# A graph network in seven edge passes on one core: the steps between the passes moved into the phases beside them

## What is computed

```python
h = relu(layernorm(x)); x = x + clip(h + segment_sum(h[src] * edge_weight * weight, dst) + 0.1 * h, 0, 1)
h = relu(layernorm(x)); x = x + tensor_product_layer(h, edge_attr_8, ...)     # sums over src
h = relu(layernorm(x)); x = x + segment_sum(einsum('ei,eio->eo', h[src], W_rel[type]) * e, dst)
h = relu(layernorm(x))
w = kernel_net(edge_attr_6).reshape(-1, 16, 16)                               # one 16x16 matrix per edge
for i in range(4):
    agg = segment_sum(einsum('ei,eio->eo', h[src], w), dst) * inv_deg
    h = gelu(agg + h @ root_W[i] + root_b[i])
x = x + h
```

## Time and profile before

| quantity | value |
|---|---|
| median of 3 runs | 26,634.41 us (26,603.08 to 26,652.0) |
| the profiled execution, its time | 26,617.11 us |
| its span, first to last instruction | 26,615.3 us |
| PE busy | 20,719.2 us (78%) |
| DVE busy | 19,332.0 us (73%) |
| ACT busy | 13,734.7 us (52%) |
| POOL busy | 19,283.0 us (72%) |
| mean granted TensorE clock | 0.884 |

### The profile page before, as it was taken

One profiled execution on the slowest core, in us unless ns is written; L12 is line 12 of the kernel. 1 busy time (PEld: TensorE's weight loads), 2 busy tenths in 40 slices (PEclk: granted clock), 3 DMA queues, 4 the chain that ended last, 5 costly groups with the idle time before them and its releaser, 6 DMA issues. The chain is left out here.

```text
span 26615.3 us, 414978 instructions
## 1 busy us (share of the span) xinstructions
PE 20719.2 (78%) x124290; PEld 13265.2 (50%) x124290; DVE 19332.0 (73%) x31590; ACT 13734.7 (52%) x14669; POOL 19283.0 (72%) x17673
## 2 busy tenths in 40 slices
PE   5777738888885888885888888588886888778886
PEld 2333326666653444443444444466664666556664
DVE  5555537777775777775777777688886888778886
ACT  4666601111112555553222222588886888778885
POOL 5777758888884666665777777677776777767776
PEclk9888968888887999997888888799997999889998
DMA  2222235555552222221333333466664666556664
GB/s 46 42 41 42 40 65 91 93 93 93 92 91 53 63 62 62 62 63 47 118 118 119 118 117 119 124 177 179 177 171 132 179 176 177 147 155 179 178 177 123
DMA packets 2209937, 2929.13 MB, mean 110 GB/s; under 512 B 979092, under 2 KB 1694178, under 8 KB 2182118
## 3 DMA queue, kind: packets, MB, share of 16 engines
q1 hardware_dynamic: 1250178, 2311.22, 29.5%
q0 software_dynamic: 814208, 166.54, 9.4%
q10 hardware_dynamic: 145440, 450.17, 4.4%
HBM read 2252.13 MB, written 674.06 MB: 110 GB/s over the span
## 5 line engine op out<-in xcount | busy, mean ns | idle before, releaser
L601 POOL DMA_INDIRECT got<-table,idx x14746 | 14929.0, 1012 | 6026.9 <-issue 4434.6
L778 PE MATMUL in_place<-place_hot,tparts 128*128 128x320 bf16 (+1 forms) x63408 | 11225.5, 338 | 2420.8 <-ACT place_hot L954 2420.7
L778 PEld LDWEIGHTS in_place<-place_hot,tparts 128*128 128x128 bf16 x63408 | 6449.6, 104 | 6568.0 <-ACT place_hot L954 2716.6
L949 ACT ACTIVATE near<-place_b,far_lanes 128x640 bf16<-128x640 f16 (+1 forms) x9180 | 6302.8, 771 | 216.8 <-DMA place_b<-place_row 216.3
L1087 DVE TENSOR_REDUCE msg<-prod 128x64 f32<-128x1024 f32 x4040 | 4906.8, 1215 | 103.3
L954 ACT ACTIVATE place_hot<-near,one 128x5760 bf16<-128x5760 bf16 (+1 forms) x1020 | 4805.9, 4712 | 33.2
L1454 POOL DMA_INDIRECT added<-add_rows,add_idx x2222 | 3690.9, 1661 | 766.2 <-issue 617.6
L1079 DVE TENSOR_TENSOR prod<-w_in,got 128x1024 f32<-128x1024 f32 x2424 | 2913.4, 1222 | 695.8 <-DMA got<-table,idx 580.6
L939 ACT ACTIVATE outb<-run 128x256 f32<-128x256 f32 (+1 forms) x1010 | 737.6, 730 | 4124.9 <-DVEq L1124 4124.9
L1497 PE MATMUL acc<-hot,spread 128*128 128x392 bf16 x12120 | 2399.1, 352 | 0.0
L890 ACT ACTIVATE h<-h1p,b 128x512 f32<-128x512 f32 x808 | 544.3, 686 | 2682.5 <-DVE wcopy L1072 2544.4
(11 more groups left out here) (253 smaller groups left out, 17587.0 us busy)
## 6 DMA issues: line engine op xcount, KB each, us to landing
w_in<-kept SPq DMA_DIRECT2D x2424, 512.0 KB, 3.3
kept<-wcopy ACTq DMA_DIRECT2D x808, 512.0 KB, 2.7
got<-table,idx POOLq DMA_INDIRECT x14746
attr<-in_edge_attr SPq DMA_DIRECT2D x202, 1024.0 KB
rows<-in_src_row SPq DMA_DIRECT2D x202, 704.0 KB
sums<-outb SPq DMA_DIRECT2D x1010, 128.0 KB
place_b<-place_row SPq DMA_DIRECT2D x612, 160.0 KB
range_b<-range_row SPq DMA_DIRECT2D x609, 160.0 KB
```

The lines of the kernel that those rows point to most:

```text
L601: pool.indirect_dma_start(out=dst[:, j * width:(j + 1) * width], out_offset=None, in_=table, in_offset=bass.IndirectOffsetOnAxis(ap=idx[:, ...
L778: mm = pe.matmul(in_place[b][:, h, :], tparts[:, s, t, :], place_hot[:, b, t, h * XC:(h + 1) * XC], start=(t == 0 and s == 0), stop=(t == ...
L949: act.activation(near[:, t, :], place_b[:, b, :], ACT.Abs, bias=SB["far_lanes"][:, t:t + 1]).then_inc(S["near_made"], 1)
```

## The change

The changed program differs in five places:

- `root_rows` is gone. Its transposes, copies and matmuls stand in `collect`, on PE and DVE, behind the mending of the carried rows, for each of the four depths. The bias `root_b` is added by the last instruction of a block, which was a copy.
- `table_parts` is gone. The edge pass loads the table into `rows` (a tile that exists already) and DVE splits it inside the pass's phase, ahead of its first `pick`; PE waits for `parts_made` before its first sums.
- SP issues the indices of chunks 0 and 1 first in a pass, then places and ranges, then the 13 loads of the table.
- `sum_unsorted` is one phase with both groups of features and the turning in it, behind one jump.
- `node_update_3` works in two halves of 784 columns, without the addition of the bias, and SP stores each half of the table as soon as its gelu is made. The table of depth 0 is stored once ahead of the loop. After the last depth nothing is stored.

```diff
         layernorm(nc, SB)
+        store_table(nc, h, table16)
         for depth in range(DEPTH):
-            root_rows(nc, SB, depth)
-            store_table(nc, h, table16)
             edge_pass(nc, a, SB, "kernel_kept" if depth else "kernel_net", table16)
-            collect(nc, SB, sums16, D)
+            collect(nc, SB, sums16, D, depth)
             sum_unsorted(nc, a, SB, sums16, D)
-            node_update_3(nc, SB, depth)
+            node_update_3(nc, SB, table16 if depth < DEPTH - 1 else None)
...
# edge_pass
-            table_parts(nc, table, tparts)
+            whole = SB["rows"][:, 0:KT * P].rearrange("p (t c) -> p t c", t=KT)
+            table_v = table.rearrange("(o r) f -> r o f", o=OWNERS)[:, :, 0:D]
...
+                def load_whole():
+                    sp.wait_ge(S["whole_clear"], 1)
+                    for t in range(KT):
+                        w = min(P, RANGE - t * P)
+                        sp.dma_start(whole[0:w, t, :].rearrange("r (o f) -> r o f", o=OWNERS), table_v[t * P:t * P + w, :, :]).then_inc(S["whole_in"], 16)
...
+                for k in range(2):
+                    load_idx(k, k, 0, k)
                 if X:
                     load_places(0, 0)
                     load_places(1, 1)
                     load_ranges(0, 0)
-                for k in range(2):
-                    load_idx(k, k, 0, k)
+                    load_whole()
...
# PE, ahead of the first in_place_sums
+                    pe.wait_ge(S["parts_made"], 1)
...
# DVE
+                def split_table():
+                    dve.wait_ge(S["whole_in"], 16 * (KT))
+                    c = Chain(dve, S["whole_step"])
+                    c.step(dve.tensor_copy(tparts[:, 0, :, :], whole[:, :, :]))
+                    for s in range(1, PIECES):
+                        c.step(dve.tensor_tensor(whole[:, :, :], whole[:, :, :], tparts[:, s - 1, :, :], ALU.subtract))
+                        c.step(dve.tensor_copy(tparts[:, s, :, :], whole[:, :, :]))
+                    dve.sem_inc(S["parts_made"], 1)
+
                 if X:
                     for b in range(HALVES):
                         hot_rows(b, b, 0)
+                    split_table()
                     pick(0, 0, 0)
...
# collect, PE
+                for n in range(BLOCKS):
+                    c0, places, w = blockwise(n)
+                    if n >= 2:
+                        pe.wait_ge(taken, n - 1)
+                    pe.transpose(pt[n % 2][0:w, :], h[:, c0:c0 + w], SB["ident"][:, :]).then_inc(turned_p, 1)
+                    pe.wait_ge(turned_s, n + 1)
+                    pe.matmul(pz[n % 2][:, 0:w], hT[0:w, n % 2, :], SB["bd_root"][0:w, depth, 0:w], start=True, stop=True).then_inc(mapped, 1)
...
# node_update_3
+            for n in range(2):
+                qs, cols = slice(n * HALF, (n + 1) * HALF), slice(n * HALF * D, (n + 1) * HALF * D)
+                dve.tensor_tensor(..., bcast(SB["inv_deg"][:, qs], 2, D), ALU.mult).then_inc(scaled, 1)
+                dve.wait_ge(scaled, n + 1)
+                dve.tensor_tensor(tmp[:, cols], tmp[:, cols], agg[:, cols], ALU.add).then_inc(summed, 1)
...
+                act.activation(h[:, cols], tmp[:, cols], ACT.Gelu_apprx_tanh).then_inc(made, 1)
...
+                sp.wait_ge(made, n + 1)
+                sp.dma_start(table.rearrange("(p q) f -> p (q f)", p=P)[:, cols], h[:, cols]).then_inc(stored, 16)
```

More of the change, by code:

```diff
@@ L446, in _ @@
                 dve.tensor_copy(range16[:, :], own[:, :]).then_inc(made, 1)
[L449 to L472, removed]
 def relation_weights(nc, a, SB):
@@ L978, in _ @@
                 early = 2
+                if X:
+                    dve.memset(whole[:, KT - 1, :], 0.0).then_inc(S["whole_clear"], 1)
                 dve.memset(run[:, 1, :, :], 0.0).then_inc(S["run_cleared"], 1)
@@ L1200, in _ @@
                 dve.wait_ge(carried, 1)
-                dve.tensor_tensor(fixed[:, :], fixed[:, :], carry[:, :], ALU.add).then_inc(fix_made, 1)
+                dve.tensor_tensor(fixed[:, :], fixed[:, :], carry, ALU.add).then_inc(fix_made, 1)
+                if depth is None:
+                    return
+                for n in range(BLOCKS):
+                    c0, places, w = blockwise(n)
+                    dve.wait_ge(turned_p, n + 1)
+                    if n >= 2:
+                        dve.wait_ge(mapped, n - 1)
+                    dve.tensor_copy(hT[0:w, n % 2, :], pt[n % 2][0:w, :]).then_inc(turned_s, 1)
+                    dve.wait_ge(mapped, n + 1)
+                    dve.tensor_tensor(tmp[:, c0:c0 + w].rearrange("p (q f) -> p q f", f=D), pz[n % 2][:, 0:w].rearrange("p (q f) -> p q f", f=D),
+                                      bcast(SB["root_b"][:, depth, :], 1, places), ALU.add).then_inc(taken, 1)
             @block.gpsimd
@@ L2076, in node_update_3 @@
[L2076 to L2080 removed]
+def node_update_3(nc, SB, table):
+    h, tmp, agg = SB["h"], SB["tmp"], SB["agg"]
+    HALF = NQ // 2
+    with phase(nc, "scaled", "summed", "made", "stored") as (block, scaled, summed, made, stored):
         @block.vector
         def _(dve):
[L2083 to L2086 removed]
+            for n in range(2):
+                qs, cols = slice(n * HALF, (n + 1) * HALF), slice(n * HALF * D, (n + 1) * HALF * D)
+                dve.tensor_tensor(agg[:, cols].rearrange("p (q f) -> p q f", f=D), agg[:, cols].rearrange("p (q f) -> p q f", f=D),
+                                  bcast(SB["inv_deg"][:, qs], 2, D), ALU.mult).then_inc(scaled, 1)
+                dve.wait_ge(scaled, n + 1)
+                dve.tensor_tensor(tmp[:, cols], tmp[:, cols], agg[:, cols], ALU.add).then_inc(summed, 1)
@@ L2088, in _ @@
         @block.scalar
         def _(act):
-            act.wait_ge(summed, 1)
-            act.activation(h[:, :], tmp[:, :], ACT.Gelu_apprx_tanh).then_inc(act_step, 1)
+            for n in range(2):
+                cols = slice(n * HALF * D, (n + 1) * HALF * D)
+                act.wait_ge(summed, n + 1)
+                act.activation(h[:, cols], tmp[:, cols], ACT.Gelu_apprx_tanh).then_inc(made, 1)
+        @block.sync
+        def _(sp):
+            if table is None:
+                return
+            for n in range(2):
+                cols = slice(n * HALF * D, (n + 1) * HALF * D)
+                sp.wait_ge(made, n + 1)
+                sp.dma_start(table.rearrange("(p q) f -> p (q f)", p=P)[:, cols], h[:, cols]).then_inc(stored, 16)
+            sp.wait_ge(stored, 32)
```

257 lines of the change are left out of this document (132 added, 125 removed).

## The result

| quantity | before | after |
|---|---|---|
| median (range) | 26,627.75 us (26,603.08 to 26,652.0; 4 runs) | 26,463.57 us (26,443.72 to 26,474.75; 4 runs) |
| the profiled execution, its time | 26,617.11 us | 26,473.86 us |
| its span | 26,615.3 us | 26,472.1 us |
| mean granted TensorE clock | 0.884 | 0.883 |

A forecast was written before the change was run, and what follows sets the result against it. POOL's gathers were taken to bound the weighted and kept passes, PE and DVE the relational one, with serial gaps between. Terms summed to 206.8 us off 26,617.1, giving 26,410; forecast 26,420 us, range 26,380 to 26,475.

The forecast's parts named there:

- Update, root map and store: Three gaps ahead of kept passes: update to next phase falls from 31.7 to 9.4 us, saving 66.9 us in all.
- Depth 0: Root map of depth 0, gelu's end to the store: 20.1 us, of which one 1.0-us boundary remains, saving 19.1 us.
- the last depth: Last update to final add: the node update shrinks from 7.0 to 4.6 us, saving 2.4 us.
- Table split, passes that POOL bounds: Three kept passes and the weighted one: POOL starts earlier by 87.8 us, less 10 for held gathers, net 77.8.
- the slower rival: Kept passes: POOL's gathers are held longer throughout; doubled hits would add 720 us, giving 27,130; chance 0.03.
- Table split, relational pass: The relational pass follows PE, which would start 20.2 instead of 33.6 us into the phase, saving 13.4 us.
- General sums: After collecting, six calls: eight jumped phases fewer at 3.4 us each, saving 27.2 us.
- the passes follow DVE: Rival, kept and weighted passes: they move with the first product, gaining 55.6 us instead of 77.8; 26,432 us; chance 0.12.
- the one phase costs what all did: Rival, general sums: the single phase costs as much as all before, so 27.2 us are missing; 26,438 us; chance 0.05.
- the signs named for a wrong prediction: A kept pass changing by over 10 us, POOL waiting for a slot, or the gap after collecting staying at 17 us.
- the first two rivals: Passes following DVE (chance 0.12) and one general-sums phase costing what all did (0.05); both together 26,460 us.

The follow-up runs named there:

- gaps_only_again: Changed kernel with the edge passes, table split and general sums of the kernel before: 26,559.47 us, ratio 0.997 to the kernel before.
- split_only_again: Kernel before with only the new edge pass (indices first, table split inside the pass): 26,574.56 us, ratio 0.9979 to the kernel before.
- Late indices: Changed kernel with SP's first two index loads moved behind the table loads: 26,492.76 us, ratio 0.9947 to the kernel before.

## Why the prediction held, and where it was wrong

**Update, root map and store** held: 69.8 us for 66.9. The gap from update to next phase is 7.9 us instead of the 9.4 costed, three times; the 31.7 us it had before were read from the last gap, and the other two had 30.8 and 31.1, which takes 1.5 us back. The four half instructions and the second half of gelu took 4.8 us from first start to last end (the sum: 4.6); the store with its boundary took the rest, 3.2 us, as the first half leaves while the second is made. `gaps_only_again` shows the same 8 us with the old passes, so it belongs to this part. Depth 0 (19.3 for 19.1) and the last depth (2.2 for 2.4) held too.

**Table split, passes that POOL bounds.** Each step inside the pass came as said: first gather 2.4 to 3.1 us into the phase (2.4), PE at 20.3 to 21.3 (20.2), no wait for a slot, and each subtraction holding one gather, by 1.0 to 1.75 us (1.98 to 2.69 against 0.94). With the gather that met the first cast that is 3.2 to 4.0 us a pass, 14.8 in the four, where 10 were taken. The Trainium skill (GPSIMD Engine Reference, Specifications) names DVE instructions with two SBUF inputs, or in a 2-port perf mode, as what GpSimd contends with; the subtractions agree, and the gather that began 0.27 us ahead of the first cast took 1.41 us, which is 0.47 more than usual and near the 0.4 that the prediction reckoned for a cast if it counted (0.41 to 0.85 at this place in the five passes with a split). For the kept passes the term was 57.9 and gave 52.0 (70 in `split_only_again`): right within the wander. The step that failed is the unspoken one behind all of it, that **a pass from first gather to last stays as long as it was**. In the weighted pass 975 ns a gather became 983, 20.2 us over 2,424 gathers (3.6 of them the split's), which ate the gain of the earlier start. The prediction had looked for such holding only in the kept passes and under `prod`, as the slower rival.

**Table split, relational pass.** "It follows PE" gave 13.4 us. PE did start 12 us sooner, and in `split_only_again`, at the old step, the pass ended 19.3 us sooner after the start of its phase. In the changed kernel the pass took 24 us more from first `picked` to last, by the slower step (0.17 us over all 202 chunks would be 34; the first chunks of the kernel before were not at 19.63 either), and so ended 11.8 later. What the term said of PE's start was right; that the pass's step would stay was not.

**General sums**: 27.2 was costed and 18.2 came. The step that failed is "Two phases cost 6.8 us, one 3.4", and with it "I take the whole, because a jump over either of today's bodies is in the same average": the average was over 5.1 and 1.8. The reading of SP's waits that was to confirm it had divided 4.6 us by two, where the two waits are 4.0 and 0.6. Merging takes the turning phase from a call with 16 features, 1.7 to 1.9 us and 3.2 in the last, and two turnings and one sums phase from the relational one, 8.4 to 8.8: by these rows of the kernel before some 19 us. The gaps shrank by 1.0 to 1.9 us at four calls, 4.0 at the last and 8.5 at the relational layer.

**The rivals.** That the passes follow DVE is out: POOL waits for "issue" alone. Late indices cost 20 to 29 us in the medians, and 12 in the profile of the weighted pass, which agrees but would not prove it. That the one phase costs what all did is out: 5.1 to 5.3 us for 6.8 and for 13.7; yet most of the 6.8 us stayed, and in four of the six calls the gap shrank by only 1.0 to 1.9 us where 3.4 were costed. The slower one is out for the kept passes, at 1.051 to 1.054 us a gather against 1.048 to 1.053 before; it is the right mechanism for the weighted pass, at 8 ns instead of the 31 from which it turns the sign. Of the signs named for a wrong prediction one came: the kept passes changed by 6, 4 and 12 us from first gather to last, and the last of them oversteps the bound of 10, which was narrower than the wander of the same code. POOL never waited for a slot, and the gaps after collecting were 15.3 to 16.9 us, where 14 were forecast and 17 would have been no gain.

That the median lies inside the range, 11 us from its upper end, is in part luck: that end was set where the first two rivals hold, and neither did. What filled the room was the passes' own wander, which the sum had put at nothing.

## What to carry to other kernels

Serial steps between phases can be costed to a few us from one timeline, and moving them under a cover that is idle pays in full. A pass that repeats a chunk 200 times can't: 0.1 us a chunk in how two engines fall against each other is 20 us, as much as what an earlier start brings, so put the wander of the pass (here 10 to 20 us each, seen in code that no edit touches) into the range, ahead of any finer argument. A phase that is jumped over can cost 5.1 us or 1.8 by what lies behind the jump, so read each by itself, and not the mean: merging two saved the cheaper one.

## What the runs showed of the hardware

- The same kernel took 26.6 thousand us on some chips and 33.8 on others; there PE issues single matmuls with 1.2 to 2.4 us between them in the rows shown, behind the first 45 of a pass. The change was worth the same share on both (0.9938 and 0.9923, with intervals that overlap).
- A gather of 0.94 us that began under a 1.89-us subtraction of two SBUF operands lasted up to 2.69, to 1.2 us beyond the subtraction's end. Under the small `place_hot` one-hot tiles of the weighted pass the price was 0.006 us a gather on average before and 0.09 after.
- Of two phases that all engines jump over, the one with the large body took 4.9 to 5.3 us and the one with the small body 1.7 to 1.9; PE's branch took 3.3 to 3.8 us of the first and 0.24 of the second.
- The relational pass has two steady steps, 19.63 and 19.80 us a chunk. In the slower one PE runs more matmuls at the 1.2 GHz level after waits of about the same length (45 slow starts in 20 chunks against 54 to 88).
